# Idle products on TensorE in the attention-norm and feed-forward parts of a fused vision block

## The reference, cut to what matters

```python
hcab = conv3x3(gelu(conv3x3(ln(x), cab1_w) + cab1_b), cab2_w) + cab2_b
a = sigmoid(relu(hcab.mean((2, 3)) @ ca1_w.T + ca1_b) @ ca2_w.T + ca2_b)
x = x * skip_scale2 + hcab * a[:, :, None, None]     # layer 0 ends
t = tokens(x)                                        # (4096, 96) per image
n = ln(t)
q, k, v = heads(n @ Wqkv + bqkv)                     # 6 heads of 16
t = t + (q @ k.T * 16 ** -0.5) @ v @ Wff + bff       # no softmax
h = relu(qlinear(ln(t), W1, b1))                     # fp8 (e5m2) factors, f16 sums
t = t + qlinear(h, W2, b2)
```

## Time and profile before

| | |
|---|---|
| median of 3 runs | 12431.7 us |
| the profiled execution | 12431.3 us |
| its span, first to last instruction | 12429.5 us |
| TensorE (PE) busy | 8718.8 us, 70% |
| VectorE (DVE) busy | 11020.4 us, 89% |
| ScalarE (ACT) busy | 7823.5 us, 63% |
| GpSimd (POOL) busy | 9754.4 us, 78% |
| mean granted TensorE clock | 0.784 |

### The profile page before, as it was taken

The page is one execution under the profiler, slowest core; times in us unless marked ns, Lnnn a source line. Parts: engine busy times, 40 slices in busy tenths (PEclk is TensorE's granted clock), DMA queues, the critical chain, the costliest instruction groups (busy, mean ns, idle before and its releaser), DMA issues. The chain is left out here.

```text
span 12429.5 us, 118414 instructions
## 1 busy us (share of the span) xinstructions
PE 8718.8 (70%) x25368; PEld 2449.2 (20%) x25368; DVE 11020.4 (89%) x7214; ACT 7823.5 (63%) x11780; POOL 9754.4 (78%) x4212
## 2 busy tenths in 40 slices
PE   8866666666666666666666666666666666588887
PEld 2321111111111111111111111111111111223222
DVE  6769999999999999999999999999999999554544
ACT  6756666666666666666666666666666666355555
POOL 0039999999999999999999999999999999112120
PEclk9977777777777777777777777777777777788888
DMA  3368888888888878888888888878888887433341
GB/s 105 109 159 183 183 183 180 182 183 183 180 181 181 182 179 183 183 183 180 183 183 183 180 182 181 181 179 183 183 183 183 185 184 157 103 96 84 80 101 28
DMA packets 569246, 2013.70 MB, mean 162 GB/s; under 512 B 82134, under 2 KB 87030, under 8 KB 553974
## 3 DMA queue, kind: packets, MB, share of 16 engines
q1 hardware_dynamic: 568566, 2006.60, 70.8%
HBM read 1599.46 MB, written 406.85 MB: 161 GB/s over the span
## 5 line engine op out<-in xcount | busy, mean ns | idle before, releaser
L845 POOL TENSOR_TENSOR dBu<-rep,BC 128x1024 f32<-128x1024 f32 x3072 | 7152.8, 2356 | 841.5 <-DMA rep<-dd_dram 835.1
L628 PE MATMUL py<-hC,fold 128*32 128x512 f32 x12288 | 2955.9, 860 | 2479.6 <-POOL hC L852 1935.1
L805 DVE TENSOR_TENSOR_SCAN pd<-pd,dBu 128x1024 f32<-128x1024 f32 x2048 | 4670.8, 2281 | 15.9 <-POOL dBu L845 6.6
L676 ACT ACTIVATE pd<-rep,a_now 128x1024 f32<-128x1024 f32 x3072 | 3419.9, 1113 | 930.1 <-DVE hC L813 742.8
L813 DVE TENSOR_TENSOR hC<-pd,BC 128x1024 f32<-128x1024 f32 x2048 | 2507.4, 1224 | 159.9 <-DVE pd L805 26.3
L852 POOL TENSOR_TENSOR hC<-h,BC 128x1024 f32<-128x1024 f32 x1024 | 2403.1, 2347 | 251.7 <-DVE h L805 249.4
L805 DVE TENSOR_TENSOR_SCAN h<-pd,dBu 128x1024 f32<-128x1024 f32 x1024 | 2333.5, 2279 | 24.3 <-ACT pd L676 24.3
L688 ACT ACTIVATE carry<-pd 128x1 f32<-128x1 f32 x1536 | 262.0, 171 | 2080.5 <-DVE hC L813 2063.6
L628 PEld LDWEIGHTS py<-hC,fold 128*32 128x32 f32 x12288 | 521.6, 138 | 4685.7 <-POOL hC L852 2727.1
L1449 POOL TENSOR_TENSOR p_y<-p_y 96x1024 f32<-96x1024 f32 x56 | 134.4, 2431 | 1152.8 <-DMA p_y<-y_dram 1152.8
L597 PE MATMUL pp<-xdbl,w_dt 38*96 38x512 f32 x1024 | 690.5, 807 | 369.3 <-ACT xdbl L705 366.8
(11 more groups left out here) (151 smaller groups left out, 8583.2 us busy)
## 6 DMA issues: line engine op xcount, KB each, us to landing
rep<-dd_dram SPq DMA_DIRECT2D x1024, 768.0 KB, 12.2
BC<-bc_dram SPq DMA_DIRECT2D x2048, 256.0 KB, 9.2
u<-u_dram SPq DMA_DIRECT2D x128, 768.0 KB, 5.4
dd_dram<-LG SPq DMA_DIRECT2D x256, 384.0 KB, 5.2
dd_dram<-RL SPq DMA_DIRECT2D x256, 384.0 KB, 3.5
y_dram<-y SPq DMA_DIRECT2D x256, 384.0 KB, 11.9
p_y<-y_dram SPq DMA_DIRECT2D x61, 1536.0 KB, 15.8
u_dram<-p_u SPq DMA_DIRECT2D x32, 1536.0 KB, 7.6
```

Source lines behind the costliest of these rows:

```text
L628: last = mm(py[32 * g:32 * g + 32, t2(t)], fold[:, :], hC[:, j % 2 * 3 + g, t2(t)], start=(j % 4 == 0), stop=(j % 4 == 3), skip_group_chec ...
L676: go(pd[:, i % 2, :], rep[:, half, 0, g, :], ACT.Exp, scale=a_now[:, i:i + 1]).then_inc(S.exped, 1)
L805: v.tensor_tensor_scan(turned(dst, k), turned(pd[:, i % 2, :], k), turned(dBu[:, i % 4, :], k), 0.0, ALU.mult, ALU.add).then_inc(S.scanned, 1)
L845: nc.gpsimd.tensor_tensor(dBu[:, i % 4, :], rep[:, half, 1, g, :], BC[:, s, 0, r, :], ALU.mult).then_inc(S.dbu, 1)
```

## The change

A product `idle_product` is added, of 96 × 32 weights (the first tap of cab1) with 512 columns of XL, float32, into rows 96 to 127 of bank 2, which nobody reads. It waits for nothing and signals nothing. It is issued three times behind the last product of the channel gate, twice per tile in the attention norm and twice per tile in the feed-forward part: 35 times an image.

```diff
                 mm(ps[0:C, 4, 1:2], ca2[:, :], hidden[:, :], start=True, stop=True).then_inc(S.ca_done, 1)
 
 
+                def idle_product():
+
+                    mm(ps[96:128, 2, :], cab1[:, 0, :], XL[:, 0:WS, 0:W], start=True, stop=True,
+                       skip_group_check=True)
+
+                for _ in range(3):
+                    idle_product()
+
...
                     if 1 <= i <= NT:
                         turn(i - 1)
                     if i < NT:
+                        idle_product()
                         var_t(i)
                     if i >= 2:
                         add_gram(i - 2)
+                    if i < NT:
+                        idle_product()
...
                 for i in range(NT + 2):
                     if i < NT:
                         center_f(i)
+                    if i < NT:
+                        idle_product()
                     if 1 <= i <= NT:
                         up(i - 1)
                     if i + 1 < NT:
                         attend(i + 1)
                     if i < NT:
                         var_f(i)
+                        idle_product()
                     if i >= 2:
                         down(i - 2)
```

## The result

| | before | after |
|---|---|---|
| median | 12429.4 us (4 runs beside it) | 12636.5 us (4 runs) |
| span of the profiled execution | 12429.5 | 12636.7 |
| ratio, 95% interval | | 1.0165 [1.0148, 1.0183] |

The kernel became slower by 207 us. The forecast was 12480 us, slower by 49: right in sign, four times too small, and outside the range of 12375 to 12530.

The account below looks back on a forecast made before the run. A ring through TensorE, ScalarE and VectorE was taken to bound norm tiles, and one through the Y1 copy feed-forward tiles; 12431.3 + 42 (norm) + 7 (feed-forward) = 12480 us, range 12375 to 12530.

Parts of the forecast that it names:

- What bounds a tile: Norm tile: the larger of the waiting loop, 4.61 us with the change, and TensorE's work, 4.88 us, decides.
- The ring of the earlier trace: Norm tile before: `turn`, `var_t`, log and exponential on ScalarE, VectorE multiply, next `turn`; 3.57 us at 2.4 GHz.
- Price of one product: One idle product beside its neighbours: between near zero and 1.04 us at 2.4 GHz; 1.04 taken.
- the upper end: Idle product in series with a shape change on each side: 0.86 + 2 × 0.09 = 1.04 us.
- The clock: Norm stretch: 2.4 GHz from about 5 us after the last gate product, and it stays.
- Norm tiles: Norm stretch with two idle products per tile: 46.1 against 40.9 us, +5.2 an image, +42 us over eight.
- The three products at the start: Behind the last gate product: they end at about 4.8 us, making `center_t(0)` 1.4 us late.
- Feed-forward: Feed-forward stretch: +3.7 us of tile work against clock gain, 57.3 against 56.9; +0.9 an image, +7 over eight.
- Side by side: Rival, both stretches: idle products cost about nothing beside 96-column ones; −56 us, 12375; chance 0.16.
- break-even: Rival, both stretches: price 0.86 us without shape changes; +1.5 us an image, 12443; chance 0.13.
- The clock does not rise: Worst rival, both stretches: 32-column products count for less than 38-column ones; some 65 us an image more, 12950; chance 0.03.
- later-rise case: Rival, norm stretch: one more slow tile an image, about 9.5 for 4.9 us; +37 more, 12517; chance 0.10.

Follow-up runs that it names:

- wide_off_ring: Kernel before plus 96-column idle products into bank 7, three at the norm start and one per norm tile behind `add_gram`; 12416.8 us, ratio 0.9993.
- start_narrow6: Kernel before plus six 32-column idle products in a row at the norm start, none in tiles or feed-forward; 12417.3 us, one run.
- norm_only: The full change without both idle products of the feed-forward loop; 12533.1 us, ratio 1.0076.
- ff_only: The full change without the three idle products at the norm start and both of the norm loop; 12508.5 us, ratio 1.0067.
- start_cab: Kernel before plus 96-column idle products, three at the norm start and five in the pause inside cab2; 12387.9 us, ratio 0.9967.
- norm_four32: The full change without feed-forward idle products, each norm one made four 32-column products side by side in bank 7; 12540.5 us, ratio 1.0093.

## Why the prediction was right or wrong

**What bounds a tile.** Right for this change. The ring of the earlier trace rows and TensorE's own work of 2.80 us decided as laid out, and the switch from ring to work came: 2.80 + 2 × 1.11 = 5.02, measured 5.03. Not complete, though: the second ring, through `center_t` and the square, was missing, and it set the tile of wide_off_ring.

**Price of one product.** Right in kind: in series, the upper end. The size was 1.04 and is 1.11 us (0.07 × 16 = 1.1 us a norm stretch). By the starts of the single passes each change comes 0.09 us late, as forecast, and the second pass behind it is late too, by 0.03 us for a narrow product and 0.08 for a wide one. At a change the first weight load begins only together with its product (both at 11313.58), where in the kernel before a load can begin well ahead of its product (at 11259.42 for the one at 11259.84).

**The clock.** This is the step that failed: "With the added products TensorE has hardly a pause in the stretch, so I expect it to be at 2.4 GHz from about 5 us after the last gate product on." It came up 29 us after it, at 1.2 GHz for 27.3 us of each stretch, with the engine busy throughout, because the idle products alternated with products of another shape. The prediction had named this sign of being wrong, a clock still at 0.50 behind the third tile: `var_t(2)`, at 11302.26, still ran at 1.2 GHz. The evidence was read too broadly. The earlier trace rows shows eight passes of *one* shape in a row; it shows that few columns are enough, and start_narrow6 confirms that, but it says nothing on narrow passes between wide ones. The 0.09 us of the earlier trace rows was used as a price and not as what it also is, a pause in the stream. The runs show that the changes of shape matter more for the clock, 12.0 us a stretch (57.4 against 45.4), than for the price, some 4 us (16 × 0.25). The Trainium skill (TensorEngine Tiling (Array Packing), Key Properties) says that a change of the tiling mode drains the engine; the late starts agree with it in kind, and the prediction cited it for the price alone.

**Norm tiles.** Predicted 46.1 us a stretch, measured 57.4. Where the clock held, norm_only took 45.4 us for the same instructions. So the sum was sound, and the 11.3 us an image, 90 of the 157 us by which the total was missed, came from the clock (57.4 − 45.4 = 12.0 us an image between held and fallen). That 46.1 is so close to 45.4 is in part luck: the price was 0.07 us too low for each of 16 products, and against that stood a late start that was put too high and a short fall of the clock that the held stretch did not have.

**The three products at the start.** 1.4 us late was forecast; it is 0.8 (4.1 us from the gate product to `center_t(0)`, 3.3 before). A small error the other way.

**Feed-forward.** Predicted +0.9 us an image, measured +8.3. Two terms. I left 11 us at 1.2 GHz and there were 24.6. And I priced a slow microsecond at 0.25 us, from stretches in which a ring through ScalarE was the bound; with TensorE as the bound it costs about half a microsecond. ff_only shows it: its stretch of 72.5 us had 37.4 slow and those of 65.7 had 24.7, which is 6.8 / 12.7 = 0.54. 13.6 × 0.5 = 6.8 of the 7.4 us missed. The tile, 6.06 us (up at 11361.68 and at 11367.74), was forecast at 5.95.

**Left out.** The y-norm behind it, which the prediction put at nothing: +1.2 us an image. It has some 16.7 us at 1.2 GHz in seven of the eight images, and had that in only two before.

**The rivals.** Side by side and break-even did not happen. "The clock does not rise" was given 0.03 and ruled out with the earlier trace rows; the truth was a mild form of it, by another cause than the column count that I named, and the later-rise case was sized at one slow tile where there were three.

## What to carry to other kernels

Idle products can pay: a few of them, of the same shape as their neighbours, in a wait that is already there, and only until the clock is up (here −0.22% for 3 per image, −0.52% for 14). Put into the tiles, they lengthened every tile at 2.4 GHz, by 0.6 us (one wide product), 0.9 (two wide) and 1.5 (two narrow), also where the clock was up. And a narrow product between wide ones should be checked for both effects of the change of shape, the time and the pauses.

## What the runs showed of the hardware that was not expected

Full busy time is no sign of full activity: 4.00 us busy of 4.00 at a granted clock of 0.50 for more than 20 us, with start-to-start times 11% over those of an unmixed stream. The same instruction stream has two durations, 45.4 and 57.4 us, by whether the clock fell just behind its beginning; filling one pause (start_cab) can move that moment. Raising the clock and keeping it were different things here: it stayed at 1.00 at 72% busy in start_narrow6 and at 0.50 at 100% busy in after. That the mixing of shapes and not the width keeps the clock down is shown by start_narrow6 (narrow, not mixed, 3.4 us slow) and norm_four32 (four column groups, mixed, 27.3 us slow). That it does so through the pauses is argued, and how long a pause may be was not tried.
